# Attention: the exchange of the two halves of queries and keys, by a product with a permutation matrix or by sixteen SBUF-to-SBUF transfers

## The reference, cut to what matters

```python
def _rotate_half(x):
    x1, x2 = (x[..., :x.shape[-1] // 2], x[..., x.shape[-1] // 2:])
    return jnp.concatenate([-x2, x1], axis=-1)
...
q = q * cos + _rotate_half(q) * sin
k = k * cos + _rotate_half(k) * sin
scores = jnp.einsum('bqhd,bkhd->bhqk', q, k) / jnp.sqrt(jnp.float32(D))
```

## Time and profile before

| what | us |
|---|---|
| median of 3 runs | 3073.23 |
| lowest and highest run | 3072.82, 3077.64 |
| span of the profiled execution (core 0) | 3085.3 |
| the attention stage in it, from its first load to the next stage's first | 987 to 1658 |
| PE, DVE, ACT, POOL busy over the span | 2554.8, 2009.3, 1671.0, 1351.2 |

### The profile page before, as it was taken

The page is one execution under the profiler, slowest core; times in us unless marked ns, Lnnn a source line. Parts: engine busy times, 40 slices in busy tenths (PEclk is TensorE's granted clock), DMA queues, the critical chain, the costliest instruction groups (busy, mean ns, idle before and its releaser), DMA issues.

```text
span 3085.3 us, 39824 instructions
## 1 busy us (share of the span) xinstructions
PE 2554.8 (83%) x12734; PEld 1552.1 (50%) x12796; DVE 2009.3 (65%) x3911; ACT 1671.0 (54%) x2533; POOL 1351.2 (44%) x1024
## 2 busy tenths in 40 slices
PE   7778878878855589999986999995889997677997
PEld 4445545545544245555553666663344444455775
DVE  1688888888788567878762222223877886456547
ACT  3788778778774145555543111112787787333542
POOL 0788888788884222111101000003455442443770
PEclk9899999999976789999997999997988999688999
DMA  3587877888885666555524100002010000414666
GB/s 117 111 169 150 179 165 144 177 172 147 174 179 135 133 181 158 94 89 91 90 37 164 47 24 25 23 14 52 7 15 8 8 8 6 166 61 145 203 190 226
DMA packets 154874, 330.46 MB, mean 107 GB/s; under 512 B 20176, under 2 KB 98896, under 8 KB 152624
## 3 DMA queue, kind: packets, MB, share of 16 engines
q0 software_dynamic: 38752, 164.36, 24.1%
q1 hardware_dynamic: 115920, 163.56, 22.1%
HBM read 173.48 MB, written 169.12 MB: 111 GB/s over the span
## 4 chain that ended last, share of the span: by engine, by line
PE 39%; issue 8%; DVE 8%; ACT 5%; POOL 4%; DMA 3%; SPq 0%; POOLq 0%; DVEq 0%; ACTq 0%
PE PS L1678 6%; PE PS L1972 3%; PE PS L1700 3%; PE PS L2016 3%; PE PS L2543 2%; PE PS L2558 2%; PE PS L1341 2%; POOL rows_z L2843 2%; PE PS L2034 2%; PE PS L1269 1%; PE PS L1299 1%; DMA rows_z<-Z 1%; PE PS L1323 1%; PE PS L1320 1%; DVE PS L1529 1%
## 5 line engine op out<-in xcount | busy, mean ns | idle before, releaser
L858 POOL TENSOR_TENSOR Z<-Z 128x1024 f32<-128x1024 f32 x256 | 645.2, 2723 | 130.9 <-DVE Z L759 77.8
L766 DVE TENSOR_TENSOR_SCAN Z<-PS,Z 128x1024 f32<-128x1024 f32 x256 | 576.7, 2277 | 21.7 <-POOL Z L858 11.6
L537 PE MATMUL PS<-Z 128*128 128x128 f32 x2048 | 305.3, 295 | 122.4 <-DVE Z L766 48.2
L537 PEld LDWEIGHTS PS<-Z 128*128 128x128 f32 x2048 | 250.9, 151 | 256.2 <-issue 85.9
L686 ACT ACTIVATE PS<-Z 128x511 f32<-128x511 f32 x512 | 332.9, 687 | 61.7 <-DVE Z L766 59.8
L1437 ACT ACTIVATE Z<-PS 128x512 f32<-128x512 f32 x320 | 188.9, 597 | 253.7 <-PE PS L1323 250.7
L1529 DVE CUSTOM_DVE_ANT_0 PS<-PS,Z 128x512 f32<-128x512 f32 (+3 forms) x512 | 242.3, 512 | 125.5 <-PE PS L1299 121.2
L698 ACT ACTIVATE Z<-PS,Z 128x512 f32<-128x512 f32 x378 | 246.1, 684 | 83.0 <-PE PS L537 79.0
L2102 ACT ACTIVATE Z<-Z 128x2048 f32<-128x2048 f32 x128 | 250.0, 1996 | 33.6 <-PE PS L2016 21.8
L489 PE MATMUL PS<-Z 128*128 128x512 f32 x512 | 246.2, 610 | 10.0 <-ACT Z L606 9.3
L1678 PE MATMUL PS<-Z 128*128 x560 | 248.3, 596 | 0.6 <-issue 0.4
(11 more groups left out here) (348 smaller groups left out, 5262.1 us busy)
## 6 DMA issues: line engine op xcount, KB each, us to landing
sums<-Z POOLq DMA_DIRECT2D x112, 768.0 KB, 8.1
Z<-rows_b SPq DMA_DIRECT2D x128, 256.0 KB, 4.8
Z<-scr SPq DMA_DIRECT2D x256, 128.0 KB, 7.8
rows_n<-in_L_ffn_expert_wv POOLq DMA_DIRECT2D x32, 528.0 KB, 7.4
Z<-rows_e SPq DMA_DIRECT2D x64, 258.0 KB, 3.0
scr<-Z SPq DMA_DIRECT2D x32, 384.0 KB, 3.8
Z<-rows_z SPq DMA_DIRECT2D x6, 2048.0 KB, 9.8
Z<-Z POOLq DMA_DIRECT2D x14, 768.0 KB, 7.8
```

The lines of the kernel that those rows point to most:

```text
L537: ins = e.transpose(self.turned[i % 2][:, c * 128:(c + 1) * 128], self.h(k, c // 2)[:, c % 2, i * 128:(i + 1) * 128], ident)
L766: e.tensor_tensor_scan(h, a, h, 0.0, ALU.mult, ALU.add).then_inc(s["scan"], 1)
L858: e.tensor_tensor(self.h(k, f), self.du[b % 2][:, 2 * f:2 * f + 2, :], b3(self.Bs[k % 2], 1, [128, 2, 512]), ALU.mult).then_inc(s["hin"], 1)
```

## The change

The permutation matrix, its load, the `swap` step on PE and its PSUM bank go. In their place SP issues sixteen transfers from SBUF to SBUF per quarter, each of 8 partitions by 512 fp32 (16 KB): partitions 8x to 8x+7 of `kr` receive partitions 8(x^1) to 8(x^1)+7 of the sine part. They all count on one new semaphore, and `swapped` waits for 16 times 16 of it, then adds the cosine part into `kr` in place. In `PREP`, `swap` stands in the step of `turned`, and `swapped` three steps after it instead of two; what follows is one step later, and so is the first load.

```diff
     PREP = (
...
-        (1, ("turned", 0)), (2, ("swap", 0)), (3, ("swapped", 0)), (4, ("high", 0)), (5, ("rest", 0)),
-        (6, ("middle", 0), ("heads", 1)), (7, ("low", 0), ("turned", 1)), (8, ("swap", 1)), (9, ("swapped", 1)),
...
+        (1, ("turned", 0), ("swap", 0)), (4, ("swapped", 0)), (5, ("high", 0)), (6, ("rest", 0), ("heads", 1)),
+        (7, ("middle", 0), ("turned", 1), ("swap", 1)), (8, ("low", 0)), (10, ("swapped", 1)),
...
-    EARLY = -26
+    EARLY = -25
...
-        e.dma_start(self.swap, d["swap"]).then_inc(s["d_w"], 16)
...
+        def swap(b, j4):
+            g = 4 * b + j4
+            e.wait_ge(*self.ring.done(self.uses["heads", b, j4]))
+            if g >= 2:
+                e.wait_ge(s["p3"], g - 1)
+            for x in range(16):
+                e.dma_start(self.kr[g % 2][8 * x:8 * x + 8], self.t1[8 * (x ^ 1):8 * (x ^ 1) + 8, 1, :]).then_inc(s["d_ts"], 16)
...
-        def swap(b, j4):
-            e.wait_ge(*ring.done(self.uses["heads", b, j4]))
-            e.matmul(bank("swap", b, j4), self.swap, self.t1[:, 1, :], start=True, stop=True).then_inc(s["prod"], 1)
...
         def turned(b, j4):
             r = self.uses["heads", b, j4]
             if b or j4:
-                e.wait_ge(*ring.done(self.uses["swap", b - (j4 == 0), (j4 - 1) % 4]))
+                e.wait_ge(s["swapped"], 4 * b + j4)
...
         def swapped(b, j4):
-            g, r = 4 * b + j4, self.uses["swap", b, j4]
-            e.wait_ge(*self.made["swap", b, j4])
+            g = 4 * b + j4
+            e.wait_ge(s["d_ts"], 256 * (g + 1))
             e.wait_ge(*ring.done(self.uses["heads", b, j4]))
-            if g >= 2:
-                e.wait_ge(s["p3"], g - 1)
-            e.tensor_tensor(self.kr[g % 2], self.t1[:, 0, :], ring.buf(r), ALU.add).then_inc(*ring.over(r))
+            e.tensor_tensor(self.kr[g % 2], self.t1[:, 0, :], self.kr[g % 2], ALU.add).then_inc(s["swapped"], 1)
```

More of the change, by code:

```diff
@@ L1084 @@
         (-5, ("flip",)), (-4, ("flipped",)), (-3, ("taps", 0)), (-2, ("taps", 1)), (0, ("heads", 0)),
-        (1, ("turned", 0)), (2, ("swap", 0)), (3, ("swapped", 0)), (4, ("high", 0)), (5, ("rest", 0)),
-        (6, ("middle", 0), ("heads", 1)), (7, ("low", 0), ("turned", 1)), (8, ("swap", 1)), (9, ("swapped", 1)),
[L1087 to L1090, removed]
+        (1, ("turned", 0), ("swap", 0)), (4, ("swapped", 0)), (5, ("high", 0)), (6, ("rest", 0), ("heads", 1)),
+        (7, ("middle", 0), ("turned", 1), ("swap", 1)), (8, ("low", 0)), (10, ("swapped", 1)),
+        (11, ("high", 1)), (12, ("rest", 1), ("heads", 2)), (13, ("middle", 1), ("turned", 2), ("swap", 2)), (14, ("low", 1)),
+        (16, ("swapped", 2)), (17, ("high", 2)), (18, ("rest", 2), ("heads", 3)),
+        (19, ("middle", 2), ("turned", 3), ("swap", 3)), (20, ("low", 2)), (22, ("swapped", 3)),
+        (23, ("high", 3)), (24, ("rest", 3)), (25, ("middle", 3)), (26, ("low", 3)), (32, ("values", 0)),
         (33, ("valued", 0), ("values", 1)), (34, ("valued", 1)))
-    EARLY = -26
+    EARLY = -25
     CONSTS = -45
@@ L1100, in __init__ @@
         self.wq = ar.take([2, 768])
-        self.swap = ar.take([128])
         self.wp = ar.take([2, 256])
@@ L1127, in __init__ @@
         self.s = {n: m.sem("b_" + n) for n in (
-            "d_w", "d_sel", "ready", "moments", "rstd", "once", "hn", "prod", "hc", "hi", "sub", "mid", "p3",
+            "d_w", "d_sel", "d_ts", "swapped", "ready", "moments", "rstd", "once", "hn", "prod", "hc", "hi", "sub", "mid", "p3",
             "sc", "max", "rows", "mhi", "mrest", "mmid", "mlow", "st", "exp", "pv", "yq", "yb", "ys", "yt", "yf", "pj",
@@ L1133, in __init__ @@
         for step in self.steps + [("route", NB - 1, p) for p in range(Route.PIECES)]:
-            if step[0] in ("heads", "swap", "values") or step[0] == "route" and step[2] in (6, 8):
+            if step[0] in ("heads", "values") or step[0] == "route" and step[2] in (6, 8):
                 self.uses[step] = len(self.uses)
@@ L1241, in load @@
                                     self.d_stack[which][w % 3], 16)
-        self.walk(low=low, load=load)
+        self.walk(swap=swap, low=low, load=load)
     def pe(self, e):
@@ L1262, in heads @@
             if b == 0 and j4 == 0:
-                e.wait_ge(s["d_w"], 80)
+                e.wait_ge(s["d_w"], 64)
                 e.wait_ge(s["ready"], 1)
@@ L1369, in project @@
             ins.then_inc(s["pj"], 1)
-        self.walk(flip=flip, heads=heads, swap=swap, values=values, most=most, rows=rows, weight=weight, pv=pv, back=back,
+        self.walk(flip=flip, heads=heads, values=values, most=most, rows=rows, weight=weight, pv=pv, back=back,
                   feature=feature, project=project, route=self.route.pe_steps(e))
@@ L1398, in high @@
             g = 4 * b + j4
-            e.wait_ge(*ring.done(self.uses["swap", b, j4]))
+            e.wait_ge(s["swapped"], g + 1)
             if g >= 2:
@@ L2931, in _shape_constants @@
     return {"tabe": tabe, "dest": dest.astype(np.int32), "pads": pads, "upper": (p[:, None] < p[None, :]).astype(f), "tab": tab, "ident": eye, "mask": mask,
-            "swap": np.ascontiguousarray(eye[p ^ 8]),
             "sel": sel.reshape(96, 4096), "rope": rope.astype(f),
```

## The result

The changed kernel takes **3381.95 us** (median of 4 runs, 3379.29 to 3385.47) against 3074.25 us for the kernel before on the same chip (4 runs, 3072.82 to 3077.64): a ratio of 1.0989, 95% interval 1.0968 to 1.1011. The sign was forecast, the size was not: 308 us instead of 159, above the upper end of the range. One execution of experiment 8's kernel with 16 pieces took 3785.31 us at a lower granted clock (0.698 instead of 0.87); it is left out of that kernel's ratio, and that kernel's profile is of it.

A forecast was written before the change was run, and what follows sets the result against it. PE was taken to bound the kernel amid the stage, the chain through one quarter at the start. 98 us amid the stage, 36 for block 0 and 25 for block 1 made +159, median 3232 us, range 3107 to 3320.

The forecast's parts named there:

- Period = T + 4.9 us: DVE's chain from one `turned` to the next, T included: 14.0 us, against 12.5, 10.5 and 9.95 before.
- T: Time from the end of `turned` to the data being in `kr`: 9.1 us, bounds 7.0 to 11.3.
- hidden: Rival: sixteen pieces behave as one transfer, T about 3.2 us within the 4 us cover, 3053 us; chance 0.06.
- PE's lead absorbs: Rival: PE's lead absorbs the stalls amid the stage, only the start pays, +34, 3107 us; chance 0.10.
- Every series meets traffic: Rival: loads and fills keep DMA engines filled, T 13.5 us for every quarter, about 3336 us; chance 0.09.
- the spacing in T: SP's sixteen issues per quarter: 0.474 us apart, bounds 0.345 to 0.55, entering T as 15 spacings plus 2.0 us landing.
- the 16.4 forecast: Growth in us of a block amid the stage: +1.5, +3.5, +8.4 and +3; +98 us for six blocks.
- Split on ACT and POOL ... also nothing: The split on ACT and POOL moves one step with `swapped`, hidden behind the units that follow: nothing.
- After quarter 3, "+3": DVE returns to the units 10.7 us after `turned`, PE has 6.6 us of work: +4, less 1 for the product.
- The start: Blocks 0 and 1, longer quarter periods and series behind the first load: +36 us (30 to 44) and +25 (17 to 35).
- The steps themselves: `swapped` and what follows standing one step later, apart from the transfers: nothing.
- The break-even "at T near 5 to 6 us": The change neither gains nor loses amid the stage when T is near 5 to 6 us.

The follow-up runs named there:

- experiment 8: Third and fourth quarter's steps 6 units later: against the changed kernel with 16 pieces, 3392.8 us; the same shift with two pieces of 64 partitions, 3155.11 us.
- experiment 5: Changed kernel with the same sixteen pieces of 8 partitions read from a table in DRAM, the exchange left out: 3251.77 us, ratio 1.056.
- experiment 3: Changed kernel with `high` of the first quarter and the three operations behind it one step later: 3369.51 us, ratio 1.095.
- experiment 2: Changed kernel with eight pieces of 16 partitions per quarter from SP instead of sixteen of 8: 3234.75 us, ratio 1.0513.
- experiment 4: Kernel before, product kept, with only the moved steps of the changed kernel and no transfers: 3094.68 us, ratio 1.006.
- experiment 7: Changed kernel with each series as two pieces of 64 partitions from SP: 3161.82 us, ratio 1.0275.

## Why the prediction was wrong

**Right in kind.** The chain ran as told: all `swapped` wait for a DMA, DVE's order holds `most` behind them, PE waits for DVE, PE ceases to be the bound. "Period = T + 4.9 us" gives 17.0 us with the measured T of 12.1; measured are 16.1 in the second quarter, which meets no load, and 23.1 in the third, where 18.0 + 4.9 = 22.9. The rival *hidden* fell: no issue was under 0.624 us. *PE's lead absorbs* fell as well. *Every series meets traffic* came nearest in number (3336) but not in cause: three of four series met no load, and their T is 12.1 to 12.4 us in the block shown, by their own issues. Its side remark, that PE's longer idle times could lower its clock, came true (1.00 to 0.76 amid the stage).

**The step that failed first: the spacing in T.** The prediction took 0.474 us because "the nearest row is a back-to-back series on SP". That series reads DRAM. The pieces were issued 0.666 us apart, beyond the upper end of 0.55; the landing, counted from the start of the last issue as in the prediction, was near the 2.0 taken (12.05 - 15 x 0.666 = 2.06 us). The nearest row shared the queue and the count but not the source, and experiment 5 shows that the source is what counts. With T = 12.1 instead of 9.1, each period is 3 us longer, and in the third quarter T is 18.0 instead of 13.5. There SP began 2.8 us late (1672.93 to 1675.75; 2.7 reckoned, from a second series put at 14.7 us after the first where its own period says 14.0), the 15 spacings took 10.0 us instead of 7.1, and the last piece landed 5.2 us after its issue began, where the sum left 3.7. Together, three times 3 and once 4.5, these are 13.5 of the 20.4 us by which a block came out longer than the 16.4 forecast.

**"Split on ACT and POOL ... also nothing"** failed: `high` waits in ACT's list, with the eviction behind it that frees the bank for the next `heads`. 4.3 us a block; experiment 3 takes 3.8 off that period and 4 off the block.

**After quarter 3, "+3"** failed: PE's lead was to give back 6.6 us. `swapped` came 13.4 us after `turned` (4 before), and from there to the next `turned` took 35.4 us, as before (35.5), so nothing came back. That is 3 us a block more than T explains. Whether PE's clock is the reason was not tried alone, but the rows set it a limit. The same stretch, from `swapped` to the next `turned`, in the changed kernel and in that of experiment 2 (columns as in the earlier trace rows):

```profile
1708.10:1743.60 35.50, 32.23 (x231) 19.73 (x231) 29.85 (x107) 15.88 (x31) 3.54 (x3) 0.91 0.51 82
```

```profile
1578.30:1612.10 33.80, 29.98 (x231) 18.90 (x231) 29.55 (x105) 15.79 (x31) 3.57 (x3) 1.00 0.54 87
```

With a granted clock of 1.00 all through, and as many matmuls, it is only 1.7 us shorter, though behind a shorter stall. DVE is busy for 29.9 us of the 35.5, so 5.6 us at the most could be won back at any clock, not 6.6: PE's lead helps little where DVE has so much work of its own.

**The start:** +48 and +37.5 us against +36 and +25. The chain is the one told, with T = 12.1 to 12.7 instead of 9.1 (a period of 14.06 instead of 11.0) and 19.8 us of wait in block 0's fourth quarter.

**The steps themselves** were taken as free; alone they cost 18 us (experiment 4). A part of it may lie in the periods above, so it isn't added to them.

**The break-even "at T near 5 to 6 us"** holds for the quiet quarters only. In experiment 2, with T = 6.4 us, the second period is 10.4 us, as with the product (10.5). With T under 4 us (2.9 to 3.8 in block 0 of experiment 7's kernel) the kernel is still 2.75% slower, since the third series waits for the load whatever its own length, and when it is moved out of the way PE waits in its place, by its position for the load itself.

## What to carry to other kernels

Before a small product on TensorE is replaced by transfers, price the issue with a row of the same source and target, not merely of the same queue, and multiply by the pieces: the chain was 10.66 us of issues and 1.4 us from the end of the last issue to the data. Look in every engine's list at what stands behind the instruction that will wait, also in the engine that seems far off. Cover isn't free either: in this pipeline the steps moved apart to hide the transfers cost 7 us a block, more than the transfers were seen to save. A series shared among two queues was not tried.

## What the runs showed of the hardware that was not expected

An issue on SP from SBUF to SBUF takes 0.625 us (8 partitions), 0.589 (16) and 0.590 (64); of the same 8 partitions from DRAM 0.295. GpSimd's queue takes 0.484 us for 16 partitions from SBUF. So the price is one of the issue and of its source, and from SBUF hardly one of its size. The landing hardly grew with the size either: a piece of 128 KB landed in 2.5 us (median). The Trainium skill, "DMA: Bandwidth & Descriptors", section on the anatomy of one DMA, fits 2.0 us plus bytes over 436 GB/s on GpSimd's path, which by that estimate is 2.3 us for 128 KB; the median here, on SP's queue, is near it.

A series that meets a stack load lands 6 to 10 us late, whether it has 16, 8 or 2 pieces (T 18.0, 16.5 and 12.8 us, where the others have 12.1, 6.4 and under 4), and whether SP or GpSimd issues it (16.5 and 15.1). Counted from the load's first issue it had landed after 22.9, 21.2 and 20.5 us with 16, 8 and 2 pieces, after 22.7 with 16 pieces from DRAM, and after 19.9 from GpSimd's queue. The load's data fill the DMA engines for about 20 us (1546 to 1567 in experiment 2), so in all five kernels the series landed when the load's data were through or shortly behind, however short it was.
